# GpSimd sums nine row pieces between its groups of four gathers, and the groups wait for four more pieces of work each

## What is computed

```python
e = stack([tbl_f[ids[:, f]] for f in range(32)], axis=1)      # 1024 x 32 x 64
i, j = triu_indices(32, k=1)                                  # 496 pairs
left = einsum('bpd,pde->bpe', e[:, i], W)                     # W: 496 x 64 x 64
z = sum(left * e[:, j], axis=-1)                              # 1024 x 496
h = concat([z, dense_ctx], axis=1)                            # 1024 x 512
h = relu(h @ W_top1 + b_top1); h = relu(h @ W_top2 + b_top2); y = h @ W_top3
```

## Time and profile before

| | |
|---|---|
| median of 3 runs | 583.75 us (582.8 to 584.56) |
| the profiled execution | 586.02 us, of which its span is 584.1 us |
| busy in the span | PE 421.7 us (72%), DVE 333.8 (57%), ACT 331.8 (57%), POOL 294.5 (50%) |
| mean granted clock of PE | 0.88 |
| gathers | 256, 944 ns each in the record |

### The profile page before, as it was taken

How to read it: one execution, slowest core, us unless ns; L and a number is a source line. 1 busy time by engine, 2 the same in 40 slices (tenths; PEclk the granted TensorE clock), 3 DMA queues, 4 the chain that set the end, 5 groups by cost and what they waited for, 6 DMA issues and landing times.

```text
span 584.1 us, 8849 instructions
## 1 busy us (share of the span) xinstructions
PE 421.7 (72%) x2440; PEld 223.8 (38%) x2440; DVE 333.8 (57%) x289; ACT 331.8 (57%) x2479; POOL 294.5 (50%) x356
## 2 busy tenths in 40 slices
PE   0140059468857697669988789177989799999998
PEld 0030023224433343335444344043545355445546
DVE  0000047446656475556578577056688689988780
ACT  0000047368478266762574569355558689789862
POOL 6777535555544463445545434655555406667240
PEclk9985569679779797888979989678999999999999
DMA  8999401211100010011101000101101000000000
GB/s 140 170 168 163 80 12 35 68 21 20 21 14 17 19 21 15 19 19 19 20 13 22 16 16 13 25 19 19 20 19 21 17 3 2 2 1 2 2 1 0
DMA packets 44679, 18.86 MB, mean 32 GB/s; under 512 B 39764, under 2 KB 40280, under 8 KB 44632
## 3 DMA queue, kind: packets, MB, share of 16 engines
q1 hardware_dynamic: 36120, 8.86, 11.6%
q0 software_dynamic: 8512, 9.45, 8.4%
HBM read 18.29 MB, written 0.00 MB: 31 GB/s over the span
## 4 chain that ended last, share of the span: by engine, by line
PE 34%; DVE 7%; another core or an unknown queue 6%; issue 3%; ACT 0%; DVEq 0%; ACTq 0%
PE left L816 10%; PE left L811 10%; PE z_sum L837 5%; DVE z_nat L672 2%; DVE row_products L663 2%; PE turned L855 2%; PE turned L776 1%; PE turned L877 1%; PE left L824 1%; PE left L855 1%; DVE column_products L643 1%; DVE column_products L651 1%; DVE column_products L655 1%; PE turned L886 1%
## 5 line engine op out<-in xcount | busy, mean ns | idle before, releaser
L596 POOL DMA_INDIRECT rows<-in_tbl_dram,ids_sb x256 | 241.6, 944 | 212.5 <-DVE column_products L655 77.4
L708 ACT ACTIVATE row_products<-row_products 128x64 f32<-128x64 f32 x1200 | 287.3, 244 | 22.7 <-issue 18.0
L708 ACT ACTIVATION_READ_ACCUMULATOR row_products<-row_products 128x1 f32 x1200 | 228.4, 190 | 18.8 <-issue 18.4
L655 DVE TENSOR_TENSOR column_products<-left,X 128x1024 f32<-128x1024 f32 x104 | 125.2, 1218 | 118.0 <-remote 86.5
L663 DVE TENSOR_TENSOR row_products<-left,rows 128x1024 f32<-128x1024 f32 x120 | 143.0, 1217 | 80.5 <-remote 38.9
L816 PE MATMUL left<-w_sb,X 64*128 64x512 f32 x480 | 138.1, 669 | 68.4 <-issue 54.2
L811 PE MATMUL left<-X,w_sb 64*128 64x256 f32 x960 | 141.9, 428 | 55.9 <-DVE row_products L663 30.7
L811 PEld LDWEIGHTS left<-X,w_sb 64*128 64x128 f32 x960 | 101.2, 211 | 116.4 <-DVE row_products L663 42.8
L691 ACT ACTIVATE X<-turned 128x512 f32<-128x512 f32 (+1 forms) x34 | 19.3, 567 | 144.4 <-remote 72.7
L816 PEld LDWEIGHTS left<-w_sb,X 64*128 64x128 f32 x480 | 44.7, 201 | 114.9 <-issue 84.3
L613 POOL TENSOR_TENSOR row_products<-row_products 128x512 f32<-128x512 f32 (+4 forms) x75 | 45.4, 606 | 52.8 <-DVE row_products L663 48.1
(11 more groups left out here) (30 smaller groups left out, 80.5 us busy)
## 6 DMA issues: line engine op xcount, KB each, us to landing
rows<-in_tbl_dram,ids_sb POOLq DMA_INDIRECT x256
w_sb<-in_W_top_dram SPq DMA_DIRECT2D x1, 512.0 KB
w_sb<-in_L_rec_W_dram SPq DMA_DIRECT2D x1, 496.0 KB
w_sb<-in_L_rec_W_dram SPq DMA_DIRECT2D x1, 480.0 KB
w_sb<-in_L_rec_W_dram SPq DMA_DIRECT2D x1, 464.0 KB
w_sb<-in_L_rec_W_dram SPq DMA_DIRECT2D x1, 448.0 KB
w_sb<-in_L_rec_W_dram SPq DMA_DIRECT2D x1, 432.0 KB
w_sb<-in_L_rec_W_dram SPq DMA_DIRECT2D x1, 416.0 KB
```

Of the source, the lines that this page charges most:

```text
L596: pool.indirect_dma_start(out=rows[:, q % 2 * QT + t, f * D:(f + 1) * D], out_offset=None, in_=tables[f], in_offset=bass.IndirectOffsetOnA ...
L655: nc.vector.tensor_tensor(to, of, X[:, n:n + 2, :].rearrange("p g b -> p (g b)").unsqueeze(1).to_broadcast([P, 2, BANK]), ALU.mult).then_i ...
L708: ins = nc.scalar.activation(product, product, ACT.Copy, accum_out=z_nat[:, tile, column:column + 1])
```

## The change

`pieces_before` is now asked for each gather, and tells a number for the first of each group of four: the largest of g - 56 and, in the first quarter, (g - 16)/2, where g = 4n is the gather's number; in the first groups it is no more than the pieces that the gathers of three groups before allow (`WITHIN`). Worked out by this rule, the number of pieces that a group waits for is:

| group | 5 | 6 | 7 | 8 | 9 | 10 | 11 | 12 | 13 | 14 | 15 | 16 | 19 | 20 | 21 | 22 | 29 | 48 | 63 |
|---|---|---|---|---|---|---|---|---|---|---|---|---|---|---|---|---|---|---|---|
| before | 0 | 0 | 0 | 0 | 0 | 0 | 0 | 0 | 3 | 6 | 10 | 13 | 23 | 27 | 30 | 34 | 57 | 122 | 173 |
| after | 0 | 1 | 3 | 5 | 7 | 10 | 14 | 16 | 18 | 20 | 22 | 8 | 20 | 24 | 28 | 32 | 60 | 136 | 196 |

The planner may give a row piece w to POOL ahead of gather g, the first gather of the group that comes next by its costs when the piece is multiplied, if g is at least 64, at least 8 past the last such place, and g - w is at least 40. Nine row pieces are summed so. In POOL's program the sum stands behind the group's wait and ahead of its first gather, and waits itself for piece w. The planner's cost of a gather becomes 1.25 us each (5.0 for four before).

```diff
-GATHER, LANDING, W_FIRST, W_PAIR = 5.0, 9.5, 6.0, 0.1
+GATHER_FIRST, GATHER, LANDING, W_FIRST, W_PAIR = 3.5, 1.25, 6.0, 6.0, 0.1
-PACED, PIECES_APART = 12, 3.4
-def pieces_before(q, m):
-    n = FP * q + FP - 1 - m
-    return max(0, int((n - PACED) * PIECES_APART))
+GATHERS = 4 * FP * QUARTERS
+GROUP, AHEAD, APART, LAG = 4, 56, 1.0, 3
+FIRST_AHEAD, FIRST_APART = 16, 0.5
+def first_gather(q, m):
+    return 4 * (FP * q + FP - 1 - m)
+def within(m):
+    columns, rows = make_work()
+    return sum(min(k for k, _ in x[2]) >= m if x[0] == "columns" else x[2] >= m for x in columns[:COLUMN_PIECES]) \
+        + sum(x[3] >= m for x in rows[:ROW_PIECES])
+WITHIN = [within(FP - n) for n in range(FP + 1)]
+def pieces_before(g):
+    if g % GROUP:
+        return 0
+    n = int(max((g - AHEAD) * APART, (g - FIRST_AHEAD) * FIRST_APART if g < 4 * FP else 0))
+    if g // 4 - LAG <= FP:
+        n = min(n, WITHIN[max(0, g // 4 - LAG)])
+    return max(0, n)
+SPARE, SUM_FROM, SUM_EVERY = 40, 64, 8
...
+    def gathers_until(self, end):
+        while len(self.gathered) < end:
+            g = len(self.gathered)
+            begin = self.gathered[-1] if g else GATHER_FIRST
+            if g == first_gather(1, FP - 1):
+                begin += CHUNKS * GATHER
...
+            n = pieces_before(g)
+            if n > len(self.end):
+                return False
+            if n:
+                begin = max(begin, self.end[n - 1] + SIGNAL)
+            if g in self.summed_before:
+                begin = max(begin, self.row_end[self.summed_before[g]])
+            self.gathered.append(begin + GATHER)
+        return True
+    def sum_by_pool(self, n):
+        w = self.row_work[n]
+        g = GROUP * sum(end <= self.end[w] + GATHER for end in self.gathered[GROUP - 1::GROUP])
+        if g >= GATHERS or g < max(SUM_FROM, max(self.summed_before, default=0) + SUM_EVERY) or g - w / APART < SPARE:
+            return False
+        del self.gathered[g:]
+        self.summed_before[g] = n
+        self.pool = self.gathered[g - 1]
+        self.pool = max(self.pool, self.end[w] + SIGNAL) + ROWSUM_POOL
+        self.row_end[n] = self.pool
+        self.plan.append(("gathersum", (g, w)))
+        return True
...
         if x[0] == "rows":
-            self.waiting.append(n)
             self.row_work.append(w)
+            if not self.sum_by_pool(n):
+                self.waiting.append(n)
...
                 for m in range(FP - 1, -1, -1):
-                    if pieces_before(q, m):
-                        pool.wait_ge(multiplied, pieces_before(q, m))
-                    for t in range(QT):
-                        for f in (2 * m, 2 * m + 1):
-                            pool.indirect_dma_start(
...
+                    for n in range(4):
+                        t, f = n // 2, 2 * m + n % 2
+                        before = pieces_before(first_gather(q, m) + n)
+                        if before:
+                            pool.wait_ge(multiplied, before)
+                        if first_gather(q, m) + n in sum_before:
+                            sum_rows(sum_before[first_gather(q, m) + n])
+                        pool.indirect_dma_start(
...
+            for w in pool_sums[len(sum_before):]:
+                sum_rows(w)
```

More of the change, by code:

```diff
@@ L170, in __init__ @@
         self.fill, self.held, self.x_work = None, False, 0
-        self.end = []
+        self.end, self.gathered, self.summed_before = [], [], {}
         self.left = [0.0] * RING
@@ L186, in landed @@
     def landed(self, q, m):
[L188 to L198, removed]
+        last = first_gather(q, m) + 3
+        return self.gathered[last] + LANDING if self.gathers_until(last + 1) else None
+    def gathers_until(self, end):
[4 more added lines that the diff above has]
+                begin += CHUNKS * GATHER
+            if g in (first_gather(2, FP - 1), first_gather(3, FP - 1)):
+                before = g // (4 * FP) - 2
+                if not self.done(before):
+                    return False
+                begin = max(begin, max(e for e, x in zip(self.end, self.work) if x[1] == before) + SIGNAL)
+            n = pieces_before(g)
[11 more added lines that the diff above has]
+        if g >= GATHERS or g < max(SUM_FROM, max(self.summed_before, default=0) + SUM_EVERY) or g - w / APART < SPARE:
+            return False
+        del self.gathered[g:]
[5 more added lines that the diff above has]
+        return True
     def on_pe(self, what, begin, length):
@@ L520, in dlrm_tower @@
         act_sums = [n for what, n in plan if what == "rowsum1"]
-        pool_sums = [n for what, n in plan if what == "poolsum"]
+        sum_before = {n[0]: n[1] for what, n in plan if what == "gathersum"}
+        pool_sums = list(sum_before.values()) + [n for what, n in plan if what == "poolsum"]
         work_of_quarter = [max(w + 1 for w, x in enumerate(work) if x[1] <= q) for q in range(QUARTERS)]
@@ L577, in _, with sum_rows @@
                                     pattern=[[-1, P]], channel_multiplier=1).then_inc(ident_ready, 1)
+            halvings = 0
+            def sum_rows(w):
+                nonlocal halvings
+                x, n = work[w], rows_before[w]
+                pool.wait_ge(multiplied, w + 1)
+                z_nat_free(pool, x[1])
+                column = 16 * ROW_UNITS.index(x[3:5])
+                of = row_products[:, n % ROW_PRODS, :, :].rearrange("p o (j d) -> p (o j) d", d=D)
+                d = D // 2
+                while d:
+                    to = of[:, :, 0:d] if d > 1 else z_nat[:, x[2] % (2 * QT), column:column + 16].unsqueeze(2)
+                    ins = nc.gpsimd.tensor_tensor(to, of[:, :, 0:d], of[:, :, d:2 * d], ALU.add)
+                    if d > 1:
+                        halvings += 1
+                        ins.then_inc(halved, 1)
+                        pool.wait_ge(halved, halvings)
+                    d //= 2
+                ins.then_inc(pool_summed, 1)
             pool.wait_ge(ids_loaded, 16)
@@ L590, in _ @@
                 for m in range(FP - 1, -1, -1):
-                    if pieces_before(q, m):
-                        pool.wait_ge(multiplied, pieces_before(q, m))
-                    for t in range(QT):
-                        for f in (2 * m, 2 * m + 1):
-                            pool.indirect_dma_start(
-                                out=rows[:, q % 2 * QT + t, f * D:(f + 1) * D], out_offset=None, in_=tables[f],
-                                in_offset=bass.IndirectOffsetOnAxis(ap=ids_sb[:, QT * q + t, f:f + 1], axis=0),
-                            ).then_inc(rows_gathered[q % 2][m], 16)
@@ L601, in _ @@
[L601 to L619, removed]
+                    for n in range(4):
[6 more added lines that the diff above has]
+                        pool.indirect_dma_start(
+                            out=rows[:, q % 2 * QT + t, f * D:(f + 1) * D], out_offset=None, in_=tables[f],
+                            in_offset=bass.IndirectOffsetOnAxis(ap=ids_sb[:, QT * q + t, f:f + 1], axis=0),
+                        ).then_inc(rows_gathered[q % 2][m], 16)
```

## The result

The changed kernel takes 628.28 us (median of 4 runs, 623.25 to 630.6) against 584.15 us (4 runs of the kernel before): 1.074 times as long, 95% interval 1.067 to 1.081. Forecast were 614 us and a range of 550 to 648. An execution more than 1.5% above the fastest of its kernel is left out of the times compared here; only the kernel of experiment 1 had such, two of its four on chip A.

The account below looks back on a forecast made before the run. Gathers issued in a row were taken to hold up all engines, longer bursts costing more per gather. Part 1 +34, the start -4 and the rest 0 gave +30 on the median 583.75: 614 us, range 550 to 648.

Parts of the forecast that it names:

- the stalls are not of the gathers' making: Rival: something else in step with gathers holds the engines, so bunching and spreading don't matter; 584 us, chance 0.08.
- The prices: Time beyond 1.49 us a piece, per four gathers: alone 1.72 us, pairs 2.59, twelve in one go 2.83, sixteen 4.09.
- Where the sums stand: Gathers 116 to 250: nine sums at g - w of about 40, some 16 gathers apart, each making POOL wait.
- the signs that were named: Nine POOL waits of 10 to 20 us ahead of sums, 12 to 20 gathers behind each, long DVE gaps.
- part 1: Group 22 and later: gathers bunch behind waiting sums, 133 us against 98.9; +34 us, bounds +4 and +56.
- Part 2, the start: Up to piece 34: first gathers spread, then 28 in one go from 96 us; -4 us, bounds -11 and +10.
- Faster: the sums don't hold POOL: Rival: POOL reaches sums when their pieces are done, so groups from 22 on come alone; 553 us, chance 0.22.
- Slower still: Rival: every burst costs like the sixteen (+56) and the start is dear (+10); 650 us, chance 0.14.
- The page's rule: Skill's rule that compute and DMA can't slow each other and PE and ACT never wait; gathers wouldn't hold ACT.

Follow-up runs that it names:

- experiment 1: Changed kernel with no sums ahead of gathers, new waits kept: 553.3 us where the kernel before takes 583.7, and 429.1 us where it takes 426.0.
- experiment 4: Kernel of experiment 1, but behind the first quarter only every fourth group waits, giving bursts of sixteen gathers: 660.4 us against 583.7 for the kernel before (1.133).
- Experiment 3: Changed kernel without sums between gathers, the nine groups still waiting for the sums' pieces, planner told: 618.8 us against 583.7 for the kernel before (1.059).

## Why the prediction was right, point by point

- **What bounds the kernel.** "Gathers, one after another, hold up the others, and the longer the burst the worse" is shown for chip A by experiment 4: fours to sixteens, nothing else altered but which group waits (and the order that the planner makes of it), and 553 becomes 660 us. The rival that the stalls are not of the gathers' making asked for 584 in experiment 1, which gave 553. But the price is no slope: "the longer the burst the worse per gather" holds from eight to twelve and hardly beyond, as the next point shows. What the prediction could not see is that this holds for one chip and not for another.
- **The prices.** Groups alone were read at 1.72 us; groups 22 to 31 of the kernel after cost 1.83. Sixteen were read at 4.09; the twenty gathers of the round above cost 51.57 us less 20 pieces x 1.49, so 21.8 us, 4.35 for four; the run of 28 (from 289.9) costs 42.36 less 8 pieces, 30.4 us, 4.35 as well; regular sixteens cost 4.0. The one long run of the trace of before was a fair sample. The twelve of the earlier trace rows, at 2.83, was not: the first run of twelve behind piece 34 (from 392.5) takes 31.25 us with 12 pieces, 13.4 us, 4.46 for four.
- **The yardstick.** The 1.49 us for a piece is a little low. The rows end at 567.70 us, when piece 246 is done; the 248th ends at 568.9, so 75 pieces take 112.98 us, 1.51 each, as on chip B. It lowers each price of a group by about 0.1. For the same reason groups 22 to 63 of the kernel before cost 419.3 less 318.9, 100.4 us, and not 98.9.
- **Where the sums stand.** Worked out as g - w of about 40 and some 16 gathers apart from gather 116; they stand at 40 to 42, the first ahead of 128, and 8 to 36 apart. So the signs that were named came only in part: not 10 to 20 us of waiting at each of nine sums but 4 to 32, with two of them between 10 and 20, and not 12 to 20 gathers behind each but 8 to 36. Where the planner leaves 36 gathers, POOL catches up with its own wait and two groups come alone.
- **The price of part 1.** 35 groups x 3.46 = 121 us were set down; 32 groups cost 120.4. That the sum is right is luck: the mean per group was set too low (3.76 measured) and three groups too many were counted. The one mean also hides two prices. The 22 groups in runs of 12 to 28 cost 94.9 us, 4.3 each, and the ten in runs of four and eight 22.7, 2.3 each.
- **Part 1 as a whole.** 133 us forecast for everything from piece 34 on, 140.7 measured (459.6 less 318.9). Of the 8 us, 6 are the ten groups 22 to 31 where seven were set at a lower price (18.3 against 12), and 2 the end, where 36 pieces took 1.55 us each.
- **Part 2, the start.** Group 15 was put at 96 us and starts at 97.66. But piece 34 ends at 149.8, not at 143 to 146: not 28 but 32 gathers follow without a wait, since group 21's piece 28 is done in the free first microseconds of the run, and they cost 52.04 less 12 x 1.49 = 34.2 us where 29 were set. The -4 us became 0. PE's granted clock in the middle was to fall under 0.87 and is 0.87 from piece 34 to 212 (0.86 from 72 on), so this sign did not come.
- **The sum.** +30 forecast, 625.8 - 584.1 = +41.7 measured in the two profiles (+44.1 between the medians). From piece 34 on it is +40.3 (459.6 against 419.3) where +34 was set, the start is 0 where -4 was set, and behind the last piece 1 us is added. So the mechanism was right, and the start and the ten groups ahead of the first sum were sized too low.
- **The rivals.** "Faster: the sums don't hold POOL" named 553 us for groups that all come alone: experiment 1 is the nearest kernel to that, with eleven pairs, and takes 553.3. It was the right number for a case that didn't come, since POOL indeed comes early to the sums and waits there. "Slower still", 650, was 22 us off where the forecast was 14 off; its price for long runs (4.09) was the better one, but a third of the groups behind gather 128 came in short runs. Experiment 3 shows that it is the wait, as said, and not the summing.
- **The page's rule.** That PE and ACT never wait on anyone at SBUF's engine side (the Trainium skill, SBUF — State Buffer, "SBUF: two separate sides") fits chip B, where PE is busy 97% beside 192 gathers. It gives no reason for what chip A shows, and whether SBUF's ports have a part in that isn't shown by any run here.

## What to carry to other kernels

When one engine's instructions slow down all the others, ask in what bursts they come, and price a burst by its length from stretches of the trace: pieces done, less the pieces' own time. Work put into a queue between paced instructions brings its own wait with it: if that wait is later than the pace, everything queued behind it is released at once, and the pace is gone (72 us on 553 here, 65 of them without doing any of the work). And measure on more than one chip before tuning against such a stall: 584 and 426 us were the same program.

## What the hardware showed that was not expected

- The kernel before takes 584 us on one chip and 426 us on another, each time within 1% in its jobs. In the runs on the fast one no variant is over 1% from before but the one that clears a buffer first.
- What separates them is not the gathers themselves: 944 to 947 ns each, 1.25 us apart, on both. On chip A DVE first stops for over 3 us 4 to 13 us behind the start of a run of twelve or more gathers and, but for a few pieces, does nothing until up to 4 us behind its end; on chip B 192 in a row pass unnoticed. The cause isn't settled. No run here takes apart bytes and issuing on chip A, and none tells why PE and ACT stop with no wait that the profile shows: late instructions and blocked accesses to memory are both left open.
- On chip A runs of four and eight gathers cost the others 1.6 to 2.6 us for four on average (experiment 1 and the earlier trace rows), and runs of 12 to 28 behind piece 34 cost 4.0 to 4.5 (the kernel after and experiment 4), nearly all of the 5.0 us in which four gathers are issued.
- Single gathers with a wait each bring the kernel to 536 us on chip A (0.915) and cost 0.6 to 0.8% on chip B.
